# Summing the keys of a linear attention: a ones product per tile on TensorE instead of additions on GpSimd

## What is computed

```python
k = elu(xn @ Wk.T) + 1                 # 6250 x 256, by heads of 32
k_sum = k.sum(over the 6250 rows)      # 256 numbers
context = k.T @ v                      # per head, 32 x 32
attn = (q @ context) / max(q . k_sum, 1e-6)
```

## Time and profile before

| what | value |
|---|---|
| median of three runs | 2052.76 us |
| the profiled execution, its time | 2057.65 us |
| its span (first to last instruction on the core) | 2055.8 us |
| granted TensorE clock, mean over the span | 0.961 |
| PE busy | 1867.3 us (91%) |
| DVE busy | 1515.0 us (74%) |
| ACT busy | 1124.5 us (55%) |
| POOL busy | 233.6 us (11%) |

### The profile page before, as it was taken

How to read it: one execution, slowest core, us unless ns; L and a number is a source line. 1 busy time by engine, 2 the same in 40 slices (tenths; PEclk the granted TensorE clock), 3 DMA queues, 4 the chain that set the end, 5 groups by cost and what they waited for, 6 DMA issues and landing times.

```text
span 2055.8 us, 42478 instructions
## 1 busy us (share of the span) xinstructions
PE 1867.3 (91%) x13524; PEld 1598.8 (78%) x13524; DVE 1515.0 (74%) x4140; ACT 1124.5 (55%) x3147; POOL 233.6 (11%) x283
## 2 busy tenths in 40 slices
PE   5789998999999999999999899997789999999745
PEld 3577886888888888888888788886579999999733
DVE  7766888777777777777739877777876666666697
ACT  4574444444444444444434456666876666666527
POOL 3452001011001101110112200000000000000070
PEclk9799998999999999999999999999999999999975
DMA  5222221010110101010144122223543334334303
GB/s 135 92 87 84 95 95 41 28 34 29 31 31 29 34 26 36 28 36 26 36 144 122 45 88 112 120 101 140 171 148 109 128 127 130 111 131 127 106 0 125
DMA packets 95698, 170.38 MB, mean 83 GB/s; under 512 B 8213, under 2 KB 67369, under 8 KB 95296
## 3 DMA queue, kind: packets, MB, share of 16 engines
q1 hardware_dynamic: 66029, 84.75, 12.6%
q10 hardware_dynamic: 27248, 77.11, 11.7%
q0 software_dynamic: 2320, 7.26, 1.2%
HBM read 110.53 MB, written 58.56 MB: 82 GB/s over the span
## 4 chain that ended last, share of the span: by engine, by line
PE 64%; DVE 17%; ACT 8%; issue 8%; POOL 3%; DMA 1%; ACTq 0%; DVEq 0%; POOLq 0%
PE psum L682 27%; PE psum L836 15%; PE psum L677 7%; PE psum L793 5%; ACT scr L1142 2%; DVE scr L1523 2%; DVE scr L1726 2%; DVE bufB L1652 2%; ACT scr L1110 1%; PE psum L652 1%; DVE bufA L1856 1%; PE psum L626 1%; DVE bufA L1848 1%; DVE bufB L1743 1%; PE psum L585 1%
## 5 line engine op out<-in xcount | busy, mean ns | idle before, releaser
L1548 DVE TENSOR_TENSOR wx<-rs_buf 128x392 bf16<-128x392 bf16 (+1 forms) x1568 | 497.0, 388 | 163.2 <-PE psum L677 159.4
L682 PE MATMUL psum<-halves,counts 128*128 128x512 f32 x2401 | 599.5, 399 | 0.7 <-ACT counts L1048 0.7
L682 PEld LDWEIGHTS psum<-halves,counts 128*128 128x128 f32 x2401 | 437.4, 189 | 85.4 <-issue 0.9
L1048 ACT ACTIVATE counts<-psum 128x392 fp32r<-128x392 f32 x784 | 327.4, 507 | 273.1 <-PE psum L677 271.8
L836 PE MATMUL psum<-bufB,wx 128*128 128x125 f32 x3392 | 410.6, 279 | 17.0 <-DVE bufB L1743 12.0
L836 PEld LDWEIGHTS psum<-bufB,wx 128*128 128x128 f32 x3392 | 392.3, 192 | 35.3 <-issue 20.9
L677 PEld LDWEIGHTS psum<-wx 128*128 128x128 bf16 x3136 | 157.6, 98 | 39.2 <-issue 20.6
L677 PE MATMUL psum<-wx 128*128 128x98 bf16 x3136 | 183.9, 210 | 3.7 <-DVE wx L1548 2.5
L793 PE MATMUL psum<-bufA,wx 128*128 (+1 forms) x800 | 180.1, 376 | 3.1 <-POOL rs_buf L543 3.1
L793 PEld LDWEIGHTS psum<-bufA,wx 128*128 128x128 f32 x800 | 146.6, 188 | 20.1 <-issue 3.3
L1726 DVE TENSOR_TENSOR scr<-scr 128x125 f32<-128x125 f32 x280 | 81.2, 290 | 105.5 <-ACT scr L1142 98.8
(11 more groups left out here) (259 smaller groups left out, 2446.0 us busy)
## 6 DMA issues: line engine op xcount, KB each, us to landing
bufA<-gates_of_x ACTq DMA_DIRECT2D x136, 500.0 KB, 3.4
gates_of_x<-bufB SPq DMA_DIRECT2D x24, 1000.0 KB, 3.9
x_times_eps_plus_sums<-scr SPq DMA_DIRECT2D x50, 128.0 KB, 1.7
sums_by_feature<-scr SPq DMA_DIRECT2D x50, 128.0 KB, 1.8
scr<-x_times_eps_plus_sums SPq DMA_DIRECT2D x49, 128.0 KB, 2.0
wx<-in_x_dram SPq DMA_DIRECT2D x25, 250.0 KB
x_plus_mix<-wx SPq DMA_DIRECT2D x25, 250.0 KB, 4.5
bufB<-sums_by_feature SPq DMA_DIRECT2D x21, 250.0 KB, 3.0
```

The costliest lines, as they stand in the source:

```text
L682: return mm(psum[:, 3 + v, :], cnt[v][:, hi, :], xhl[:, hi, :, :].rearrange("p s d -> p (s d)"), start=(hi == 0), stop=(hi == NT - 1))
L1048: fn(cnt[v][:, :, c * u:c * (u + 1)], psum[:, CB[u % 4], 0:PER * KEYS].rearrange("p (c h) -> p h c", h=NT), ACT.Copy).then_inc(S["c_sb"], 1)
L1548: last = tt(to, tab2[:, 0:k_, :].unsqueeze(1).broadcast_to([P, PER // 2, k_, 2]), keysT[v][:, part_, g0:g0 + PER // 2, :].unsqueeze(2).bro ...
```

## The change

GpSimd's addition goes, and with it `k_acc`, its clearing, DVE's wait for the addition, and the product at the end. In their place PE multiplies, in each tile right behind M's products, a matrix of ones with the same keys and accumulates in the upper half of PSUM bank 1, which DVE clears at the start of the stage. The small products for the edge groups, which used bank 1, move to free columns of bank 0.

```diff
-            pool.wait_ge(S["acc_z"], 1)
             for t in range(NT):
...
                 pool.tensor_tensor(xhl[:, t, 1, :], x_ring[q % XR][:, j, :], xhl[:, t, 0, :].bitcast(F32),
                                    ALU.subtract).then_inc(S["lo_q"], 1)
-                pool.wait_ge(S["k_v"], t + 1)
-                if t:
-                    pool.wait_ge(S["acc_q"], t)
-                r = rows_of(t)
-                pool.tensor_tensor(k_acc[0:r, :], k_acc[0:r, :], k_s[t % 3][0:r, :], ALU.add).then_inc(S["acc_q"], 1)
...
                     for c in range(2):
                         last = mm(psum[:, 6, c * D:(c + 1) * D], xr(t)[0:rows_of(t), c * P:(c + 1) * P], k_s[t % 3][0:rows_of(t), :],
                                   start=False, stop=False, skip_group_check=True)
+                    last = mm(psum[:, 1, D:2 * D], ones[0:rows_of(t), :], k_s[t % 3][0:rows_of(t), :],
+                              start=False, stop=False, skip_group_check=True)
                     last.then_inc(S["m_mm"], 1)
...
-                    mm(psum[0:GB, 1, 0:NGB], tri[0:GB, :], histf[0:GB, :], start=True, stop=True)
+                    mm(psum[0:GB, 0, 128:128 + NGB], tri[0:GB, :], histf[0:GB, :], start=True, stop=True)
...
-            pe.wait_ge(S["acc_q"], NT)
-            mm(psum[:, 7, 0:D], ones[:, :], k_acc, start=True, stop=True).then_inc(S["ks_ps"], 1)
...
-            dve.memset(k_acc, 0.0).then_inc(S["acc_z"], 1)
...
-            dve.memset(psum[:, 6, :], 0.0).then_inc(S["m_z"], 1)
+            dve.memset(psum[:, 6, :], 0.0)
+            dve.memset(psum[:, 1, D:2 * D], 0.0).then_inc(S["m_z"], 1)
...
                     if t >= 3:
                         dve.wait_ge(S["m_mm"], t - 2)
-                        dve.wait_ge(S["acc_q"], t - 2)
...
             dve.wait_ge(S["m_mm"], NT)
-            dve.wait_ge(S["ks_ps"], 1)
             dve.tensor_copy(MT, psum[:, 6, :]).then_inc(S["ctx_sb"], 1)
-            dve.tensor_copy(ksum, psum[:, 7, 0:D]).then_inc(S["ctx_sb"], 1)
+            dve.tensor_copy(ksum, psum[:, 1, D:2 * D]).then_inc(S["ctx_sb"], 1)
```

More of the change, by code:

```diff
@@ L199, in build @@
         k_s = [scr[:, (3 + v) * D:(4 + v) * D] for v in range(3)]
-        k_acc = scr[:, 6 * D:7 * D]
         MT, ksum = scr[:, 0:2 * D], scr[:, 512:512 + D]
@@ L258, in build @@
             "bias_v", "eps1_v", "edge_v", "key_ok", "key_st", "oh_v", "hist_ps", "sum_ps", "idx_v", "n_ok",
-            "hi_act", "lo_q", "row_act", "row_in", "row_in2", "acc_z", "acc_q",
-            "xt_ps", "xt_A", "k_ps", "k_min", "k_exp", "k_v", "m_mm", "ks_ps", "m_z",
+            "hi_act", "lo_q", "row_act", "row_in", "row_in2",
+            "xt_ps", "xt_A", "k_ps", "k_min", "k_exp", "k_v", "m_mm", "m_z",
             "rz_v", "ctx_sb", "ctx_z", "ctx_ps", "ctx_v", "mg_ps", "mg_sb",
@@ L603, in _ @@
                     pe.wait_ge(S["idx_v"], 1)
-                    mm(psum[0:GB, 1, 0:NGB], tri[0:GB, :], histf[0:GB, :], start=True, stop=True)
-                    mm(psum[0:GB, 1, 32:32 + NGB], ones[0:GB, 0:GB], histf[0:GB, :], start=True, stop=True)
-                    mm(psum[0:GB, 1, 64:65], ones[0:EROWS, 0:GB], ecol[0:EROWS, 1:2], start=True, stop=True)
+                    mm(psum[0:GB, 0, 128:128 + NGB], tri[0:GB, :], histf[0:GB, :], start=True, stop=True)
+                    mm(psum[0:GB, 0, 160:160 + NGB], ones[0:GB, 0:GB], histf[0:GB, :], start=True, stop=True)
+                    mm(psum[0:GB, 0, 192:193], ones[0:EROWS, 0:GB], ecol[0:EROWS, 1:2], start=True, stop=True)
                     pe.wait_ge(S["idx_v"], 2)
-                    pe.transpose(psum[0:1, 1, 128:128 + GB], ecol[0:GB, 2:3], ident[0:GB, 0:GB]).then_inc(S["sum_ps"], 1)
-            pe.wait_ge(S["acc_q"], NT)
-            mm(psum[:, 7, 0:D], ones[:, :], k_acc, start=True, stop=True).then_inc(S["ks_ps"], 1)
+                    pe.transpose(psum[0:1, 0, 256:256 + GB], ecol[0:GB, 2:3], ident[0:GB, 0:GB]).then_inc(S["sum_ps"], 1)
             pe.wait_ge(S["ctx_sb"], 2)
@@ L1416, in groups_first @@
                 dve.wait_ge(S["sum_ps"], 1)
-                dve.tensor_tensor_scan(tot[0:GB, 1:NGB + 1], ones[0:GB, 0:1].broadcast_to([GB, NGB]), psum[0:GB, 1, 32:32 + NGB], 0.0,
+                dve.tensor_tensor_scan(tot[0:GB, 1:NGB + 1], ones[0:GB, 0:1].broadcast_to([GB, NGB]), psum[0:GB, 0, 160:160 + NGB], 0.0,
                                        ALU.mult, ALU.add).then_inc(S["idx_v"], 1)
-                ts(ecol[0:GB, 3:4], psum[0:GB, 1, 64:65], 0.5, None, ALU.is_lt).then_inc(S["idx_v"], 1)
+                ts(ecol[0:GB, 3:4], psum[0:GB, 0, 192:193], 0.5, None, ALU.is_lt).then_inc(S["idx_v"], 1)
                 dve.wait_ge(S["idx_v"], 4)
-                tt(idx0[0:GB, 0:NGB], psum[0:GB, 1, 0:NGB], tot[0:GB, 0:NGB], ALU.add).then_inc(S["idx_v"], 1)
+                tt(idx0[0:GB, 0:NGB], psum[0:GB, 0, 128:128 + NGB], tot[0:GB, 0:NGB], ALU.add).then_inc(S["idx_v"], 1)
                 dve.wait_ge(S["idx_v"], 5)
@@ L1428, in pass_count @@
             def pass_count():
-                dve.tensor_reduce(ecol[0:1, 6:7], psum[0:1, 1, 128:128 + GB], AX, ALU.max).then_inc(S["idx_v"], 1)
+                dve.tensor_reduce(ecol[0:1, 6:7], psum[0:1, 0, 256:256 + GB], AX, ALU.max).then_inc(S["idx_v"], 1)
                 dve.wait_ge(S["idx_v"], 8)
```

## The result

The changed kernel is a little slower: median 2057.95 us (2056.93 to 2062.41, 10 runs) against 2054.49 us (2052.18 to 2056.64, 10 runs) of the kernel before on the same chip, a ratio of 1.002 with a 95% interval of 1.0011 to 1.0028. That is +3.5 us, or 2.3 to 5.8 by the interval; the forecast was +6.7 and the stated range 2054.0 to 2063.5. In a later comparison the same pair gave 1.0017 (1.0007 to 1.0026).

A forecast was written before the change was run, and what follows sets the result against it. The stage was taken to alternate between PE back to back and PE waiting for DVE or ACT. 20 exposed products x 0.43 = +8.6, less 0.9 (end) and 1.0 (collisions), gave +6.7: 2059.5 us, range 2054.0 to 2063.5.

The forecast's parts named there:

- The term for the additions: Removing GpSimd's 49 additions frees DVE's normalisation (L1326) from collisions in DVE-bound stretches: -1.0 us.
- three exposures: One product in tile 12 to 13 and two in 16 to 18, counted as exposed at 0.43 us each.
- The price of a product: One new ones product on PE costs 0.43 us at full clock; a late tile takes 2.38 us instead of 1.95.
- the late count: Exposed products: 2 in tile 33 to 35, 2 in 38 to 40, 5 in 43 to 48, three behind 48; 0.43 us each.
- the nine in the ACT-paced stretches: Products in tiles 25 to 28, 35 to 38 and 40 to 43, around the square roots' table loads: hidden, 0 us.
- four collisions: GpSimd's additions lengthened L1326 four times in DVE-bound stretches, by 0.29, 0.19, 0.28 and 0.29 us: -1.0 us.
- DVE gains more: Rival: L1326's relief is the whole 4.4 us and on the path; sum +3.3, 2056.1 us; chance 0.08.
- its sign came: Sign in the changed profile for DVE gaining more: the stage before 63 us shorter by over 1 us.
- The first rival: Products shorten PE's waits, so falls to half clock drop out: third only +3.6 us (0.20), more than one -1.5 (0.08).
- its sign came too: Sign in the changed profile for the clock staying up: windows from 60 to 110 us well above 0.77.
- Its mechanism as I wrote it: New products shorten PE's waits of 3.69, 4.0 and 2.81 us; the length of wait the clock bears decides.
- Tile 2 to 3's product: One product between the keys' products of tiles 2 and 3, counted as exposed at 0.43 us.

The follow-up runs named there:

- products and additions: Changed kernel with GpSimd's additions, their waits and the product at the end kept, the ones products' result unused; 2063.07 us, ratio 1.0047 to the kernel before.
- filled waits: Kernel before with 4, 4 and 2 unused products in PE's waits ahead of M's products of tiles 8, 13 and 18; 2053.8 us against 2052.58.
- products where hidden: Changed kernel with GpSimd's additions instead of ones products in tiles 19 to 22, 31, 32, 36, 37, 41 to 48; 2050.75 us, ratio 0.9990 to before.

## Why the prediction was right in sign and too high in size

The total moved by +3.5 us, the forecast was +6.7, and the outcome that I had called the likeliest, over 4.1 us slower (0.66), was not the one measured. Nor is 0.2% too small to tell, as I had written: ten runs of each kernel gave 0.2% with an interval from 0.11 to 0.28%. In the stage itself the forecast was further off: the copy of M starts at 168.1 us in the mean of the three profiles of before and at 170.0 in the changed kernel, +1.9. The term for the additions was 2 us too small, the clock gave back more than 1 us that the sum did not have, and three exposures (1.3 us) were none. Another 2.0 us, in the mean of the same profiles, came behind the stage, where I had expected nothing. So the total came nearer to the forecast than the mechanism did, and that part is luck.

The forecast by its own stretches (rounded), beside the means of three profiles of each kernel (starts of the keys' products):

| stretch | forecast | measured |
|---|---|---|
| tile 2 to 3 | +0.4 | 3.83 to 4.85: +1.0 |
| tile 3 to 12 | -0.8 | 36.6 to 34.9: -1.7 |
| tile 12 to 13 | +0.4 | 3.76 to 3.28: -0.5 |
| tile 13 to 18 | +0.9 | 18.2 to 17.5: -0.7 |
| tile 18 to 21 | 0 | 10.1 to 9.6: -0.5 |
| tile 21 to 25 | +1.7 | 11.45 to 11.79: +0.3 |
| tile 25 to the copy of M | +4.0 | 59.75 to 63.1: +3.4 |
| sum | +6.7 | +1.3 |

- **The price of a product and the late count** were right: 0.43 us, 2.38 us per tile, nine exposed between tile 33 and 48, three at the end, and nothing for the nine in the ACT-paced stretches. The distance over the square root stayed at 7.86 us with the products in it. The late products are what makes the stage longer.
- **The term for GpSimd's additions was mis-sized.** I took -1.0 us from four collisions, and as bound 34 x (0.550 - 0.42) = 4.4. That bound left out the ten instructions of the line in the other buffer, whose median fell from 0.554 to 0.408 us, and it measured from 0.42, while the undisturbed line adds 18.4 / 49 = 0.375 us each to DVE's busy time (they overlap a little). DVE was relieved of over 7 us. What reached the path is read from products and additions beside the changed kernel, both with all products and at a clock of 0.94: 1.4 us in tile 3 to 12 (36.3 with additions, 34.9 without), 0.5 in 13 to 18, 0.5 in 18 to 21 and 0.6 in 28 to 33, some 3 us in all. The rival "DVE gains more", with a chance of 0.08, was the better account of this term, and its sign came: the stage before 63 us is shorter by over 1 us.
- **The clock was taken as unchanged, and it was not.** The first rival, to which I gave 0.28, came true in part, and its sign came too (0.93 instead of 0.77 from 60 to 110 us): the falls still come, but fewer and shorter. Tile 21 to 25 without products takes 12.50, 11.37 or 10.49 us in the three profiles of before, and 11.79 with them each time: 1.3 us for three exposed products at the full clock, and 1.0 us gained by the clock on average. Its mechanism as I wrote it (a shorter wait) failed in the run with filled waits.
- **Three exposures were none**, one in tile 12 to 13 and two in 16 to 18. They looked back to back only because the clock was low (4.00 and 6.88 us). In the third profile of before, where it was back sooner, they take 3.27 and 6.16 us, and with products 3.28 and 6.16. ACT sets the pace: PE waits for its copy 0.63 us at tile 13 in spite of the product, and 0.55 us at tile 18 without one.
- **Tile 2 to 3's product costs 0.9 and not 0.43**, since the clock is low there: wholly at the half clock this stretch takes 4.00 us (the second profile of before) and with a product 4.85.
- **What follows the stage was not as before.** From the copy of M to the end it is 1885.6, 1885.7 and 1881.8 us before and 1887.5, 1884.3 and 1887.3 in the changed kernel. Two places far behind the stage hold the difference. Near 1069 us PE waits 1.0, 0.7 and 1.0 us for a load of `x_plus_mix`; it has no such wait in the profiles of before. Near 1180 us, behind a wait of 3 us for GpSimd, the granted clock falls: 32 products take 7.01 us at 1.00 in each profile of before, and 8.39, 8.69 and 10.06 us at 0.82, 0.81 and 0.69 in the changed kernel's (the first profile of before, then the three changed):

```profile
1177.69 7.01 PE L793 MATMUL psum<-bufA,wx 128*128 128x250 f32 x32 [3.13 <-POOL rs_buf L543]
```
```profile
1178.41 8.39 PE L786 MATMUL psum<-bufA,wx 128*128 128x250 f32 x32 [3.02 <-POOL rs_buf L536]
1176.67 8.69 PE L786 MATMUL psum<-bufA,wx 128*128 128x250 f32 x32 [3.18 <-POOL rs_buf L536]
1177.02 10.06 PE L786 MATMUL psum<-bufA,wx 128*128 128x250 f32 x32 [3.02 <-POOL rs_buf L536]
```

Open: why these two come. The longer 32 products (8.69 us) are also in products and additions and in products where hidden, and not in the other kernels with the same later code; the load's wait is in four of the other kernels. So neither is tied to one part of the change, and three profiles a side can't tell chance from effect: the part behind the copy varies by up to 4 us between profiles of one kernel. Before tile 2 the changed kernel's three profiles are 0.6 us later in the mean (25.0 against 24.4), within the 2.3 us by which those of before differ; the cleared half bank, under 0.5 us, was not tried by itself.

## What to carry over

Count new work on a full engine stretch by stretch, at the clock and pace that the stretch will have afterwards: a stretch that is back to back only because the clock is low is no bound. Work taken off GpSimd can be worth more than GpSimd's idleness suggests, because DVE's instructions get shorter; compare their total busy time, not their merged rows. And where two engines can do the same small sum, give each tile to the one that waits there: the two kernels that did so had the shortest stages of all that form the whole sum (135.8 and 135.2 us) and lay 0.16% and 0.10% under the kernel before. In whole times the second can't be told from the kernel with seven useless products (0.11% under).

## What was not expected of the hardware

- GpSimd's 49 additions (0.72 us each) lengthened a DVE line that runs 49 times by 7 us in total, from 18.4 to 25.3 us, and the longest single one from 0.68 to 0.95 us. The Trainium skill, page "SBUF — State Buffer" (section "SBUF: two separate sides"), gives a shared port pair that one engine holds for a whole instruction. The other direction agrees best: a subtraction of GpSimd of 0.73 us took 5.05 us, to just behind the end of DVE's 4.41 us operation, and one of 6.79 us spans two of DVE in a row (1.81 and 4.42 us). The collision of the earlier trace rows is 0.27 us longer, though GpSimd's addition still ran for 0.54 us, so by these records it does not show a whole wait.
- Extra products on PE did not cost what they add: seven of them, with no use, gave a kernel 2.3 us faster (0.4 to 4.1), and the granted clock from 50 to 110 us, 0.77 to 0.83 in the kernel before, was 0.89. Nineteen of them gave -1.2 us (-3.1 to +0.6) at 0.91. The gain is small and its interval ends near nothing; that there was no loss is clearer.
